# First attention: half of the measures from chunk 6 on computed by ScalarE and GpSimd, with base terms and weight splits in other slots

## The reference, cut to what matters

```
qp = h @ Wtq.T + btq                       # two coordinates per token
diff = qp[:, :, None, :] - qp[:, None, :, :]
dist_sq = sum(diff * diff);  phase_diff = arctan2(diff[..., 1], diff[..., 0])
forward_bias = 0.5 * (1 + cos(phase_diff))
threshold = mean(dist_sq) + 1.25 * std(dist_sq)
valid = (dist_sq <= threshold) & causal
masked = where(valid * forward_bias == 0, -inf, scores)
weights = softmax(masked);  output = weights @ v @ Wo.T + bo
return h + output + 0.1 * (qp / |qp| @ Wfq.T + bfq)
```

## The kernel before, in words

| slot | measures begun in it | base part before, after | split third before, after |
|---|---|---|---|
| 0, 1, 2 | 2; none; 3 | group 1, the same | - |
| 3 | 4 | - | lot 1, - |
| 4 | 5, 6 | -, group 2 | lot 1, - |
| 5 | 7, 8 | - | lot 1, lot 1 |
| 6 | 9 | -, group 2 | - |
| 7 | - | - | -, lot 1 |
| 8 | 10 | group 2, group 2 | - |
| 9 | 11 | - | -, lot 1 |
| 10, 12 | 12; 14, 15 | group 2, - | - |
| 13 | 16 | - | lot 2, lot 2 |
| 14 | 17, 18 | - | lot 2, - |
| 15, 17 | 19; none | - | lot 2 in 15; lot 2 in both |
| 16, 18 | 20; 21 | -, group 3 | - |
| 19 | 22 | - | - |
| 20 | 23 | group 3, group 3 | - |
| 22, 24 | 25; 27, 28 | group 3, - | - |
| 25, 26, 27 | 29; 30; 31, 32 | - | lot 3, - |
| 36, 38, 40 | - | - | -, lot 3 |

## Time and profile before

### The profile page before, as it was taken

One profiled execution on the slowest core, in us unless ns is written; L12 is line 12 of the kernel. 1 busy time (PEld: TensorE's weight loads), 2 busy tenths in 40 slices (PEclk: granted clock), 3 DMA queues, 4 the chain that ended last, 5 costly groups with the idle time before them and its releaser, 6 DMA issues. The chain is left out here.

```text
span 631.6 us, 10922 instructions
## 1 busy us (share of the span) xinstructions
PE 562.6 (89%) x3508; PEld 339.2 (54%) x3508; DVE 489.2 (77%) x1428; ACT 364.7 (58%) x729; POOL 353.2 (56%) x339
## 2 busy tenths in 40 slices
PE   4987878978777998989989999899798999999996
PEld 4653555656634543545545555465555566655664
DVE  5769999996866887358577657577986999989886
ACT  4555766886335334357766877674446455545552
POOL 7578578452044537498677597453215555555553
PEclk9989898999777999889999999999989999999998
DMA  8500100000052221222012110122100000000000
GB/s 222 142 2 1 38 1 1 2 1 2 4 120 67 68 69 51 84 64 70 30 55 66 69 62 25 65 69 63 38 1 17 2 2 17 3 19 1 18 2 18
DMA packets 23425, 26.02 MB, mean 41 GB/s; under 512 B 2676, under 2 KB 13960, under 8 KB 23368
## 3 DMA queue, kind: packets, MB, share of 16 engines
q1 hardware_dynamic: 22928, 24.80, 13.6%
q10 hardware_dynamic: 440, 0.53, 0.3%
HBM read 23.09 MB, written 2.23 MB: 40 GB/s over the span
## 5 line engine op out<-in xcount | busy, mean ns | idle before, releaser
L620 POOL TENSOR_TENSOR sw<-hid,gp 128x512 f32<-128x512 f32 x64 | 81.5, 1273 | 84.6 <-DVE hid L1693 79.4
L634 POOL TENSOR_TENSOR gp<-stage,gp 128x512 f16<-128x512 f32 x72 | 83.8, 1166 | 65.4 <-ACT gp L850 65.4
L1693 DVE SCALAR_TENSOR_TENSOR hid<-stage,bank 128x512 f32<-128x512 f32 x72 | 49.3, 685 | 59.4 <-ACT stage L833 57.2
L833 ACT ACTIVATE stage<-bank 128x512 f32<-128x512 f32 x144 | 84.8, 590 | 16.3 <-PE bank L889 16.0
L570 POOL TENSOR_TENSOR row<-row,dx 128x512 f32<-128x512 f32 (+3 forms) x48 | 55.7, 1161 | 51.0 <-ACT dx L685 50.5
L785 ACT COPY ptr<-bank 128x512 f32<-128x512 f32 (+2 forms) x80 | 41.5, 519 | 73.5 <-PE bank L1088 72.4
L1103 PE MATMUL bank<-v,ptr 128*128 128x128 f32 x544 | 78.1, 285 | 4.6 <-DVE x L1511 4.6
L850 ACT CAST gp<-stage 128x512 f16<-128x512 f32 x72 | 44.5, 619 | 64.5 <-DVE stage L1756 64.5
L1204 PE MATMUL bank<-stage,wd 128*128 128x512 f32 x144 | 77.1, 618 | 5.1 <-DVE x L1700 5.1
L1103 PEld LDWEIGHTS bank<-v,ptr 128*128 128x128 f32 x544 | 71.5, 201 | 7.2 <-issue 5.9
L1739 DVE SCALAR_TENSOR_TENSOR x<-bank,comb,x 128x128 f32<-128x128 f32 x256 | 71.5, 343 | 0.1
(11 more groups left out here) (251 smaller groups left out, 1272.6 us busy)
## 6 DMA issues: line engine op xcount, KB each, us to landing
gp<-shares SPq DMA_DIRECT2D x64, 256.0 KB, 3.1
out_x<-x SPq DMA_DIRECT2D x8, 256.0 KB, 2.3
x<-in_L_attn_hidden_states SPq DMA_DIRECT2D x4, 256.0 KB, 5.1
stage<-in_L_ffn_gate_w SPq DMA_DIRECT2D x1, 576.0 KB, 4.9
stage<-in_L_ffn_up_w SPq DMA_DIRECT2D x1, 576.0 KB, 4.2
stage<-in_L_ffn_gate_w SPq DMA_DIRECT2D x1, 448.0 KB, 5.5
stage<-in_L_ffn_up_w SPq DMA_DIRECT2D x1, 448.0 KB, 3.4
row<-in_L_wmod ACTq DMA_DIRECT2D x1, 384.0 KB
```

What stands on the lines that cost most here:

```text
L620: pool.tensor_tensor(sw[:, s % 2, :], hid[:, s % 2, :], wb[:, n % HELD_WEIGHTS, :], ALU.mult)\
L634: pool.tensor_tensor(gp[:, n % HELD, 1, :], act_g[:, s % 2, :], gp[:, n % HELD, 0, :], ALU.subtract)\
L833: act.activation(sg[:, s % 2, :], gate_bank(s)[:, :], func, scale=half_of / (H_UP * W_UP))\
```

## The change

`POOL_FROM` (chunk 32) is replaced by a tuple `BY_POOL`: in batch 0 the even chunks 6, 8, ... 30 and all of 32 to 39 take the way over ScalarE and GpSimd, 21 instead of 8. `by_pool` and `pooled` follow it; batch 1 keeps its way for all chunks, with numbers that go on from 21. The parts of base group 2 begin in slot 4 instead of 8, those of group 3 in slot 16 instead of 20. The thirds of the splits come in every second slot: lot 1 from slot 5 instead of 3, lot 2 from 13 as before, lot 3 from 36 instead of 25. No other line changes; the operations themselves, their sizes and the DMAs are the same.

```diff
--- before.py
+++ after.py
@@ -95,9 +95,9 @@
 
 
 BASE_PARTS = 3
-BASE_AT = {first + every * n: (g, n) for g, first, every in ((1, 0, 1), (2, 8, 2), (3, 20, 2)) for n in range(BASE_PARTS)}
+BASE_AT = {first + every * n: (g, n) for g, first, every in ((1, 0, 1), (2, 4, 2), (3, 16, 2)) for n in range(BASE_PARTS)}
 THIRD = PIECE // 3
-WEIGHTS_AT = {first + n: (1 + lot, n) for lot, first in enumerate((3, 13, 25)) for n in range(3)}
+WEIGHTS_AT = {first + 2 * n: (1 + lot, n) for lot, first in enumerate((5, 13, 36)) for n in range(3)}
 
 
 
@@ -111,7 +111,7 @@
 LAST = ((CH - 1) * PER, BLK)
 ROUTE_PARTS = 6
 FINE = 2
-POOL_FROM = CHUNKS_BEFORE[14]
+BY_POOL = tuple(range(6, CHUNKS_BEFORE[14], 2)) + tuple(range(CHUNKS_BEFORE[14], NCH))
 LOGITS_AT = max(SPLIT_AT) + 1
 ROUTE_AT = {SLOTS - 4 - ROUTE_PARTS + n: n for n in range(ROUTE_PARTS)}
 COMB_AT = {SLOTS - CH + 1 + n: n for n in range(CH - 1)}
@@ -324,11 +324,11 @@
 
         def by_pool(b, m):
 
-            return b > 0 or m >= POOL_FROM
+            return b > 0 or m in BY_POOL
 
         def pooled(b, m):
 
-            return b * NCH + m - POOL_FROM + 1
+            return len(BY_POOL) + m + 1 if b else BY_POOL.index(m) + 1
```

## The result

The changed kernel takes 642.07 us (median of 4 runs, 640.68 to 643.06) against 634.37 us (4 runs): a ratio of 1.014, 95% interval 1.0106 to 1.0175. It is slower, by 7.7 us, and 1 us above the predicted range; the prediction had given a slower kernel a chance of 0.15. The profiled execution took 642.45 us, its span is 640.7 us (631.6 before), its mean granted clock 0.960 (0.965).

The account below looks back on a forecast made before the run. VectorE's own queue was taken as the bound up to slot 33, then VectorE, ScalarE and TensorE waiting in turn. A 2.0 us gain and 3.7 us router price gave +1.7 on 633.3: 635.0 us, range 626 to 641.

Parts of the forecast that it names:

- Ceiling and waits at chunks 10 and 12: Thirteen measures off VectorE gain at most 10.8 us; VectorE waits for GpSimd 5.6 us at chunk 10, 0.9 at 12.
- The sum of GpSimd's queue ahead of measure 10: GpSimd's work from measure 6 through measure 10 takes 18.4 us, from 60.9 to 79.3.
- The wait of 0.8 us for GpSimd at chunk 22: VectorE reaches chunk 22 at 110.0, its measure is ready at 110.8: another 0.8 us wait.
- The third lot beside the router: Nine split operations in slots 36 to 40 hold VectorE's router parts: price 3.7 us, bounds 0 to 7.6.
- a gain of 2.0 us at slot 32: Slot 32 comes 2.0 us earlier, taken between 0.4 by ScalarE and 3.6 by VectorE alone.
- Rival 1: Slower: GpSimd's queue bounds slots 4 to 22 at contended prices; +4 at slot 32, router +7.7, 641 us; chance 0.15.
- Rival 2: Faster: measures ready in time, most of 10.8 us stays, router price 0 to 3.7; 622.5 to 627 us; chance 0.18.
- Rival 3: Queues as forecast, but splits and router miss each other: no router price, 630 to 631 us; chance 0.17.

Follow-up runs that it names:

- e4: The changed kernel with the third lot of splits in slots 32 to 34: 637.76 us, ratio 1.0097 to the kernel before.
- e11: e6 with base group 2 and the first lot of splits in the change's slots: 634.49 us, ratio 1.0023 to the kernel before.
- e6: The kernel before with even chunks 6 to 20 moved, second lot in slots 21, 23, 25, third lot in 32 to 34: 626.8 us.
- e3: The kernel before with only the slots of base parts and splits changed, measures as before: 637.9 us, ratio 1.0109.
- e5: e4 with only even chunks 6 to 20 moved, 22 to 30 back on VectorE: 635.1 us, ratio 1.0024 to the kernel before.
- e7: The kernel before with only even chunks 22 to 30 moved and the third lot in slots 32 to 34: 633.89 us, ratio 0.9999.
- e8: e6 with all thirteen even chunks 6 to 30 moved: 632.58 us, ratio 0.9985 to the kernel before.
- e1: The changed kernel with only the third lot of splits back in slots 25 to 27: 639.34 us, ratio 1.0119 to the kernel before.
- e10: e4 with the second lot of splits in slots 21, 23, 25: 638.43 us, ratio 1.0097 to the kernel before.
- e12: e6 with chunks 33, 35, 37 and 39 back on VectorE: 624.94 us, ratio 0.9876 to the kernel before.

## Why the prediction was wrong

It gave 635.0 us and 626 to 641; measured 642.07. Point by point:

**Ceiling and waits at chunks 10 and 12: right, the size with some luck.** 5.6 us were predicted at chunk 10 and 5.53 measured, 0.9 and 1.40 at chunk 12. The sum of GpSimd's queue ahead of measure 10 was 18.4 us; from 62.75 to the end of measure 10 it was 17.3. Measure 6 came 1.9 us later than I took it, so measure 10 was ready at 80.0 instead of 79.3; VectorE came to it at 74.5 instead of 73.7, and the wait stayed the same. In other executions of the same queue (e4, e11) it was 3.06 us. The wait of 0.8 us for GpSimd at chunk 22 did not come: VectorE waited 0.69 us there, for TensorE. The root of slot 7 was begun at 74.80 (73.5 predicted), and ScalarE stood still for 2.91 us before it could use it, up to 76.13; VectorE waited for measure 10 until 80.0, so that this added nothing there, as predicted. e11 against e6 shows this queue as worth 7.7 us in time, 3.1 of them in the trace ahead of the mixture.

**The third lot beside the router: right.** The nine splits started at 151.87, 1.2 us behind the last measure's start, as laid out. 3.7 us predicted, 4.15 in the trace of the changed kernel, 4.2 in e3, and e3 alone is 3.9 us slower than before.

**The failed step: "a gain of 2.0 us at slot 32".** I had 3.6 us of gain by VectorE's queue, 0.4 by ScalarE's, and took the middle. In place of it stood a loss: ScalarE's exponential of slot 32 began 2.5 us late. With the router's 4.15 that makes 6.65, and the mixture began 6.67 late. What was wrong in it is the start and not the length: I gave ScalarE 19.4 us from slot 24 to slot 32, and it took 19.1. But I let it start 0.1 to 0.2 us late, and it started 3.5 late. Four things that the working had too small or left out put it there. VectorE stood 3.9 late at chunk 12 instead of 3.0. Its two root operations in slot 16 lasted 1.4 us longer: the first ended at 98.26 with a split operation (98.24), the second at 99.22 with measure 20 (99.19), the same hold that I had priced for the router and had not looked for here. In slot 19 ScalarE's new difference of chunk 22 (105.61, 0.72 us) stands ahead of its shift of the turned norm (L655), for which TensorE waited 1.74 us instead of 0.93; ScalarE in turn waited 2.03 us for TensorE ahead of the exponential of slot 21 (1.36 before), and 3.0 us late became 4.0. And from there on ScalarE had no idle time with which to catch up, while I had given it slack up to slot 24. Taking the middle between the two engines' answers had no ground either: at slot 32 VectorE was 1.0 us late and ScalarE 2.5, and by its wait for TensorE at chunk 33 VectorE became as late as ScalarE. e5 against e4 shows the late measures as a loss of 2.7 us in the change's slots, and e7 shows them worth nothing alone, where the prediction counted on 3.7 us from them. The larger loss between e8 and e6 (5.8 us, 3.9 of them in the traces ahead of the mixture) has another cause, GpSimd's queue, as told under e8.

**The rivals.** Rival 1 had the sign and nearly the time (641), but not its mechanism: GpSimd's operations did not come at contended prices ahead of measure 10 (a third took 2.7 us there), its own prices give 2.2 us more at measure 10 and not the 2.8 stated (three measures at 0.13, two thirds at 0.55 and a base part at 0.7 more), and its queue held VectorE only at chunks 10 and 12, not at 22. Rival 2 was far off. Rival 3 is refuted by e3. Two times beside the forecast were off without bearing on it: by the sum for chunk 12 lot 1 ends at 85.0, not 84, and from the end of the splits (158) to TensorE's wait (172) it is 14 us, not 12.

**What stays open.** The mixture starts 6.67 us late and the median is 7.7 late. The part behind the start of the mixture varies between 456.3 and 460.4 us over the profiled kernels, although its instructions are the same; no run tells why, and by this part alone e11 and e6 differ by 3.5 us. The mean granted clock of TensorE ahead of the mixture is 0.92 in the changed kernel, 0.95 in the kernel before and 0.97 in e6; from 76 to 83 us, around the wait at chunk 10, it is 0.56 in the changed kernel and 1.00 in the kernel before. How much of the lost time the clock adds by itself, and how much of the lower clock comes from the waits, no run separates. What the second lot's late slots are worth with the measures as before was not run either.

## What to carry to other kernels

When work is moved to an engine with a queue in order, list all that stands in that queue between the moment its input is there and the moment its result is wanted, and compare the two times; the order of that queue was worth as much here (7.7 us between e6 and e11) as the whole change. Do the same for the engine that prepares the input: where it is busy for nine tenths already, moved work has no room (ScalarE, 18.3 of 19.0 us here), and of two queues that both fill up the later one set the time. Count the buffers between the two as well: with two buffers of `dx`, a GpSimd that was late stopped ScalarE for 3.64 us in e8, and through TensorE VectorE too. Fillers without a deadline (the splits) belong where the other engine works on PSUM, and never behind a last wait that lets them run into a stretch of small SBUF operations.

## What the hardware showed that I had not expected

**The clock of TensorE can lengthen a wait on VectorE 20 us later.** The wait at chunk 10 was 5.5 us in the changed kernel, e1, e5 and e10, and 3.1 in e4 and e11, which have the same queue. What differs is TensorE's granted clock from 57 to 60 us (the first column behind the five engines' busy times), first in the changed kernel, then in e4:

```profile
57.00:60.00 3.00, 3.00 (x11) 1.73 (x11) 2.83 (x9) 1.59 (x5) 0.00 (x0) 0.53 0.00 0
```

```profile
57.00:60.00 3.00, 2.65 (x23) 2.22 (x22) 2.83 (x9) 2.93 (x7) 0.00 (x0) 1.00 0.00 0
```

0.53 is the lower of its two levels, 1.2 GHz, for nearly all of the stretch; in e4 it is 2.4 GHz throughout. At the low level the products of slot 3 took 0.61 to 0.63 us each instead of 0.38, ScalarE got its transposes later, and GpSimd began measure 6 at 62.75, in e4 at this time:

```profile
60.54 1.27 POOL L570 TENSOR_TENSOR row<-row,dx 128x512 f32<-128x512 f32 x1 [7.60 <-ACT dx L685]
```

Of these 2.2 us, 0.75 were there before the stretch (TensorE's first transpose behind its wait starts at 56.20, in e4 at 55.45), so about 1.5 us go with the clock. Behind it the queue has no gaps, and measure 10 is ready 2.2 us later; the wait is 2.5 us longer, as VectorE comes 0.3 us sooner. That it reaches the mixture's start is not shown: e10 and e5, with the long wait, start it at 175.51 and 175.68, e4 with the short one at 175.48, but their slots and chunks differ too. e6 and e12 had the low level in the same stretch, and with their shorter queue no such wait followed. TensorE had waited 2.0 to 2.1 us for VectorE just before in all of these traces, at the high level too (the kernel before, e4, e11), so that wait alone does not decide the level; what does stays open.

**A train of small operations pays one GpSimd operation each.** In the router seven of the eight rows that take 0.21 to 0.43 us when free took 0.72 to 1.05 beside splits of 0.83 to 0.96 us (the two operations of L1613 together 0.94); only L1619 went right behind L1618 in 0.24. It looks as if any gap between two such operations is enough for GpSimd to take its turn; no run took the gaps away. Reductions, the reciprocal and operations with an operand in PSUM (L1506 0.16, L1507 0.16, L1531 0.68) kept their times beside the same splits. The Trainium skill, "SBUF — State Buffer", section "SBUF: two separate sides", calls the pair of ports between VectorE and GpSimd an exclusive lock held for the whole instruction, on VectorE's side for operations in a two-port mode or with two inputs in SBUF; these rows agree with it.
